# Where a 128x1024 scan stands in VectorE's order of the attention stage

## What is computed

```
x = x + mamba(layernorm(x))
x = x + moe(layernorm(x))
x = x + attention(layernorm(x))
x = x + moe(layernorm(x))
```

```
phi_q = elu(q) + 1 ; phi_k = elu(k) + 1          # q, k, v = x @ Wq.T, x @ Wk.T, x @ Wv.T
A   = tril(phi_q @ phi_k.T)                      # inside a chunk
num = A @ v + phi_q @ S_prev                     # S_prev: sum of phi_k.T @ v over earlier chunks
den = A.sum(-1) + phi_q . Z_prev + 1e-6          # Z_prev: sum of phi_k over earlier chunks
y   = (num / den) @ Wp.T + bp
```

## Time and profile before

| | |
|---|---|
| time, median of 3 runs | 3362.16 us (3361.99 to 3362.63) |
| profiled execution, own time | 3362.63 us |
| its span | 3360.8 us |
| PE busy | 2712.3 us (81%) |
| DVE busy | 2302.4 us (69%) |
| ACT busy | 1717.8 us (51%) |
| POOL busy | 2124.2 us (63%) |
| chain that ended last | PE 40%, POOL 24%, DVE 23%, issue 8%, ACT 3% |
| turns 1 to 14 of attention | 2363 to 2857 us of the span |

### The profile page before, as it was taken

One profiled execution on the slowest core, in us unless ns is written; L12 is line 12 of the kernel. 1 busy time (PEld: TensorE's weight loads), 2 busy tenths in 40 slices (PEclk: granted clock), 3 DMA queues, 4 the chain that ended last, 5 costly groups with the idle time before them and its releaser, 6 DMA issues.

```text
span 3360.8 us, 54089 instructions
## 1 busy us (share of the span) xinstructions
PE 2712.3 (81%) x20202; PEld 1495.0 (44%) x20202; DVE 2302.4 (69%) x2483; ACT 1717.8 (51%) x3115; POOL 2124.2 (63%) x1317
## 2 busy tenths in 40 slices
PE   5787788887888778887754499996999999359998
PEld 2233334333343333343332266554666666235665
DVE  1799999999999999999996522213666666552211
ACT  3677777777777777777751122223444443122221
POOL 1899999999999999999992054433333232124442
PEclk9899999988999889998876699998999999679999
DMA  3456565565566655666542033332111111213442
GB/s 112 103 127 155 137 144 133 140 145 140 140 138 146 146 134 132 144 149 143 133 107 60 13 90 71 83 51 59 46 46 40 52 46 38 67 28 87 89 89 25
DMA packets 227392, 330.01 MB, mean 98 GB/s; under 512 B 40546, under 2 KB 116834, under 8 KB 227011
## 3 DMA queue, kind: packets, MB, share of 16 engines
q1 hardware_dynamic: 202562, 292.49, 35.3%
q0 software_dynamic: 24576, 34.10, 6.0%
HBM read 240.52 MB, written 85.98 MB: 97 GB/s over the span
## 4 chain that ended last, share of the span: by engine, by line
PE 40%; POOL 24%; DVE 23%; issue 8%; ACT 3%; DMA 1%; SPq 0%; DVEq 0%; POOLq 0%; ACTq 0%
POOL m_side L584 14%; DVE m_pair L668 8%; POOL m_hc L593 7%; PE g_h L1341 6%; PE f_h L1341 6%; PE t_wb L2056 6%; DVE m_hc L668 5%; PE f_yp L1355 3%; PE m_wk L771 3%; PE g_yp L1355 3%; DVE m_hc L677 2%; PE t_num L2056 2%; PE m_y L863 2%; PE m_pair L919 2%; DVE t_am L1978 2%
## 5 line engine op out<-in xcount | busy, mean ns | idle before, releaser
L584 POOL TENSOR_TENSOR m_side<-m_du_r,m_bc 128x1024 f32<-128x1024 f32 x416 | 975.0, 2368 | 13.4 <-DMA m_du_r<-ddd 13.1
L351 ACT ACTIVATE m_pair<-m_delta_r,m_a_neg 128x512 f32<-128x512 f32 x832 | 539.7, 681 | 179.0 <-DVE m_hc L677 128.6
L593 POOL TENSOR_TENSOR m_hc<-m_hc,m_bc 128x1024 f32<-128x1024 f32 x208 | 492.2, 2370 | 99.6 <-DVE m_hc L668 97.9
L668 DVE TENSOR_TENSOR_SCAN m_pair<-m_pair,m_side 128x1024 f32<-128x1024 f32 x240 | 547.9, 2283 | 3.4 <-ACT m_pair L351 2.8
L863 PE MATMUL m_y<-m_hc,m_fold 128*32 128x512 f32 x2048 | 321.5, 702 | 229.8 <-DVE m_hc L677 121.2
L668 DVE TENSOR_TENSOR_SCAN m_hc<-m_pair,m_side 128x1024 f32<-128x1024 f32 x176 | 397.7, 2275 | 28.6 <-ACT m_pair L351 28.6
L677 DVE TENSOR_TENSOR m_hc<-m_pair,m_bc 128x1024 f32<-128x1024 f32 x304 | 370.5, 1219 | 7.3
L771 PE MATMUL m_wk<-m_xnT,m_w_in 128*128 128x512 f32 x512 | 276.9, 668 | 10.8 <-DVE m_cw_diag L725 10.0
L771 PE MATMUL m_wk<-m_xs,m_cw_diag 128*128 128x512 f32 x512 | 244.1, 605 | 15.5 <-ACT m_xs L416 15.5
L919 PE MATMUL m_pair<-m_b_diag,m_du_t 128*32 128x128 f32 x6144 | 203.8, 289 | 43.5 <-DVE m_hc L668 24.3
L919 PEld LDWEIGHTS m_pair<-m_b_diag,m_du_t 128*32 128x32 f32 x6144 | 179.0, 117 | 124.7 <-issue 123.4
(11 more groups left out here) (308 smaller groups left out, 4887.4 us busy)
## 6 DMA issues: line engine op xcount, KB each, us to landing
m_delta_r<-ddd SPq DMA_DIRECT2D x256, 256.0 KB, 6.8
m_du_r<-ddd SPq DMA_DIRECT2D x256, 256.0 KB, 7.7
m_bc<-bcd SPq DMA_DIRECT2D x256, 128.0 KB, 2.9
ddd<-m_delta SPq DMA_DIRECT2D x32, 512.0 KB, 3.2
ddd<-m_du SPq DMA_DIRECT2D x32, 512.0 KB, 4.1
f_w<-in_w SPq DMA_DIRECT2D x24, 512.0 KB, 6.1
g_w<-in_w SPq DMA_DIRECT2D x24, 512.0 KB, 6.1
m_xt<-in_x SPq DMA_DIRECT2D x16, 512.0 KB, 10.9
```

What stands on the lines that cost most here:

```text
L351: last = nc.scalar.activation(to, delta_r[:, c % 2, q, :], ACT.Exp, scale=a_neg[:, c * NQ + q, st:st + 1])
L584: nc.gpsimd.tensor_tensor(side[:, un % RING, :, :], du_r[:, c % 2, 2 * h:2 * h + 2, :], bc[:, 0, st:st + 1, :].to_broadcast([P, 2, T]), AL ...
L593: nc.gpsimd.tensor_tensor(hc[:, un % RING, :, :], hc[:, un % RING, :, :], bc[:, 1, st:st + 1, :].to_broadcast([P, 2, T]), ALU.mult).then_i ...
L668: nc.vector.tensor_tensor_scan(to, decay, added, 0.0, ALU.mult, ALU.add).then_inc(S["scan"], 1)
```

## The change

In DVE's body of the attention stage, the call of `sum_keys` for the next batch is moved ahead of the calls of `phi` for m = 2 and 3. Its own waits (for phi of m = 0 and 1 of that batch, and for POOL's product of the batch before) go with it.

```diff
                     out_stats(b - 1, 1 - par)
                 mask(b, 1)
                 if not last:
+                    sum_keys(b + 1, 1 - par)
                     phi(b + 1, 1 - par, 2)
                     phi(b + 1, 1 - par, 3)
-                    sum_keys(b + 1, 1 - par)
                 keep2(b)
                 if ahead(b):
                     in_stats(b + 2, par)
```

## The result

The changed kernel takes 3399.7 us (median of 4 runs, 3393.35 to 3407.66), against 3362.39 for the kernel before beside it (3361.99 to 3366.5): 37.3 us more, a ratio of 1.0113 with a 95% interval of 1.01 to 1.0128. The forecast was 3402, with a range of 3393 to 3416. The four runs of the kernel before lie within 4.5 us and those of the changed one spread over 14. The record has 36 unprofiled executions of the changed kernel in all, from 3393.35 to 3410.71 us with a median of 3401.9; the twelve shortest have a mean granted clock of 0.909 over the whole execution, the twelve longest of 0.904. So the clock seems to have a part in the spread.

The account below looks back on a forecast made before the run. It took DVE's phi of slice 2, which releases PE's value matmuls in each attention turn, as the bound. Delay of 32.0 us (30.7 + 1.3) plus 8 us of clock made 40 us more: 3402 us, range 3393 to 3416.

Parts of the forecast that it names:

- The bound: In every attention turn, the start of phi of slice 2 on DVE sets when PE goes on; turns take 35.28 us.
- The delay: The scan delays phi 2 and PE's values by 2.19 us in turns 1 to 14, 1.28 in turn 0: 32.0 us.
- The second rival: A later wait in the turn partly absorbs the delay; at half the delay 3378 us, chance 0.07.
- Phi 3, the mask of block 2 and z times q at no cost: Behind the moved scan on DVE and POOL: phi 3 covered by 1.2 us, z times q by 4, mask's return worth 0.
- The clock: PE's gap before the values grows to 3.33 us; the clock falls in five turns at 1.64 us each: 8 us.
- the first rival: The delay in attention without any fall of PE's clock: 3394 us, chance 0.17.
- Third rival: PE's clock falls in every one of the 14 turns: 3417 us, or 3440 with low stretches twice as long; chance 0.13.

Follow-up runs that it names:

- e9: Changed kernel with half the scan ahead of phi 2, half behind phi 3, and four unread matmuls before the values in turns 1 to 14: 3376.8 us against 3361.13.
- e10: Against e8, the scan moved behind the mask of the state and the input norm's statistics: 3362.57 us against 3362.85 for the kernel before.
- e12: The order of e10 in turns 1 to 13 only, the kernel before's order in turns 0, 14 and 15: 3365.5 us against 3375.22 for the kernel before.
- e8: Kernel before with the output norm's four statistics instructions in pairs ahead of and behind phi 2, their aggregation ahead of the scan: 3376.23 us, ratio 1.0049.
- e3: Changed kernel with the scan put between phi 2 and phi 3: 3399.32 us, 1.0046 of the kernel before.
- e2: Changed kernel with four unread matmuls on PE ahead of the values in turns 1 to 14: 3415.09 us, 1.0092 of the kernel before.
- e1: The changed kernel again, unaltered, on a chip with long expert stages: 3423.14 us against 3384.12 for the kernel before.
- e4: Changed kernel with the scan cut in two, half ahead of phi 2 and half behind phi 3: 3414.64 us, 1.0092 of the kernel before.
- e11: The changed kernel again, unaltered, on a chip without the long expert stages: 3398.96 us against 3362.85 for the kernel before.
- e6: Kernel before with the output norm's statistics moved behind phi 3, ahead of the scan: 3417.65 us, ratio 1.0171.
- e7: Against the kernel before, scan and output statistics change places: scan ahead of the mask of block 1, statistics behind phi 3: 3385.51 us, ratio 1.0067.

## Why the prediction held, step by step

**The bound: right.** Phi of slice 2 sets when PE goes on. It shows from both sides: what delays phi 2 lengthens each turn by the delay (37.46 in the changed kernel, 36.40 in e9), and what makes it earlier shortens the turn (e10 and e12), as long as the scan doesn't hold POOL (e8). e3 leaves phi 2 alone and keeps the 1.14 us.

**The delay: right to 1 us.** 2.19 us a turn were charged and 2.18 found, turn 0's gap came out at 1.63 us for 1.64, and e2 measured the whole at 31.0 us for 32.0 (32.4 in its profiled attention stage). The second rival (partly absorbed) is out: PE's later waits of 0.33, 0.28, 0.35 and 0.44 us in turn 7 are the same to 0.01 us in both kernels.

**Phi 3, the mask of block 2 and z times q at no cost: right.** In the changed kernel none of the waits for them grew. That phi 3 had 1.2 us to spare is borne out by e3: there it starts 2.2 us further behind phi 2 than in the changed kernel, and 1.06 us of it reach the turn. The mask of block 2 came 0.2 us sooner relative to the values and not 0.3 to 0.5, for it now waits for PE; its worth of 0 stands.

**The clock: the right mechanism, about the right total, wrong number and price.** The term was five turns x 1.64 = 8 us. The runs show three, three and four turns, at 1.4 to 2.8 us each: 5.7, 5.8 and 7.2 us in the three profiles, 8.0 as e1 less e2. Fewer falls, each dearer, since the low stretch reaches past the values into the next matmuls in some turns; that the two errors cancel in part is luck, and five was a choice between none and 14. The spread of the times fits this term: the fastest of the four runs, 3393.35, is 31.0 us over the kernel before, which is the delay without a fall (the first rival's 3394), and the slowest 45.3. But these runs have no profile, so it is argued and not shown. Third rival: the clock did not fall in every turn. By the rule of the Trainium skill (TensorE: Matmul & The Clock Gate, Why this matters for your kernels) it should have; the trace disagrees, with a full clock after 11 of 14 gaps of 3.3 us. Where the step was weak is in its reason, that a gap "just below the one that fell" makes a fall a matter of length. The rows it compared don't carry that. Windows of the kernel before, over the first stage's gap of 3.38 us itself and over a longer stretch behind the gap of 4.08 us:

```profile
176.40:179.70 3.30, 0.00 (x0) 0.02 (x1) 3.27 (x3) 1.20 (x3) 3.30 (x2) 0.61 1.05 199
...
193.50:197.50 4.00, 3.62 (x28) 2.22 (x32) 3.97 (x3) 4.00 (x10) 4.00 (x2) 0.59 0.44 131
```

The clock behind the 3.38 us had already fallen early in the gap (0.61 on average over it). Behind the 4.08 us it fell as well, after the 0.7 us that the prediction looked at: 1.00 there, 0.59 over 4 us. And e4's gaps of 2.26 us fell in 8 of 14 turns, and equal gaps in one kernel did both. What else decides, these runs leave open. The profiles show 0 of 14 at 0.36, 0.53, 1.14, 1.6 (with fill) and 1.75 us, 8 of 14 at 2.26, 3 or 4 at 3.32, 14 of 14 at 5.5. I expected a rise with length and there is none between the middle ones. The turns aren't independent draws either: the falls come in two turns running (all eight of e4; 11 and 12, 8 and 9, 1 and 2, 11 and 12 in the changed kernel), but for turn 1 in two of its profiles.

**POOL: a term left out, without effect on the sum.** The prediction said that no POOL instruction moves by itself and counted for POOL only z times q. Its z times q was right (it starts 0.6 us behind the values, 0.8 predicted). But in the changed kernel POOL's 128x4 product on line 1713 falls beside the scan. The line as a group, in the kernel before:

```profile
L1713 POOL TENSOR_TENSOR t_nm<-t_nm,t_rstd x32: 200/200/209, 2288.9 to 2878.6; 128x4 f32<-128x4 f32 x32
```

and in the changed one (shortest, median and longest, in ns):

```profile
L1713 POOL TENSOR_TENSOR t_nm<-t_nm,t_rstd x32: 200/202/2277, 2298.9 to 2926.7; 128x4 f32<-128x4 f32 x32
```

In turn 2 it starts and ends with the scan (2420.52 to 2422.79). Timeline of POOL there, and of ACT, which takes the result:

```profile
2419.30 1.04 POOL L1711 TENSOR_TENSOR t_rstd<-t_ve,t_nhalf 128x4 f32<-128x4 f32 x1 [0.18 <-POOL t_nm L1709]
2420.52 2.27 POOL L1713 TENSOR_TENSOR t_nm<-t_nm,t_rstd 128x4 f32<-128x4 f32 x1 [0.18 <-POOL t_rstd L1711]
...
2425.95 2.08 ACT L1806 ACTIVATE t_xn1t<-t_xb,t_nm,t_rstd 128x256 f32<-128x256 f32 x4
```

Thirteen of its 32 executions, one in each of turns 2 to 14, take 1.98 to 2.28 us, 26.7 us more together, which is nearly all of the 27.3 us that POOL is busier in attention. (I had expected it in every turn in e11; its profile shows the same thirteen.) With half of the scan in the same place (e4) it takes just over half as long:

```profile
L1713 POOL TENSOR_TENSOR t_nm<-t_nm,t_rstd x32: 198/202/1214, 2300.7 to 2920.5; 128x4 f32<-128x4 f32 x32
```

It costs nothing in the changed kernel, because ACT takes the factors only at 2425.95, 3.2 us after they are ready. In e8 the same thing decided the result, and in e6, against e7 with its statistics as late, it has a large part in it.

## What to carry to other kernels

Before moving a long instruction in an engine's order, find which instruction of that engine another one waits for without slack: here 2.19 us ahead of phi 2 cost 31 us, 2.2 us ahead of phi 3 cost 15, and behind the statistics the scan cost nothing in turns 1 to 13 but 2.2 us in turn 0. Price a new gap on TensorE as a chance, with a range from none to all turns, and not by a threshold in its length; when you read the clock from a row, look inside the gap and well behind it too. Test it by filling the gap with unread matmuls; that splits delay and clock in one run. Look also at what the moved instruction will run beside, on other engines: a tiny instruction can be held for the whole of a long one.

## What the runs showed of the hardware

A small POOL instruction on SBUF that falls beside DVE's scan ends only with the scan: 2.27 us for 0.20 (line 1713, changed kernel), 1.21 us beside the half scan of 1.21 us (e4), 2.00 and 2.11 us for 0.24 (line 1708, e8 and e6), and 0.24 again in e7 and e10, where the scan stands elsewhere. The Trainium skill (SBUF — State Buffer, SBUF: two separate sides) says that VectorE, with two inputs in SBUF, and GpSimd take one pair of ports in turns, each for a whole instruction. The traces agree; the scan reads two tiles in SBUF, and beside the mask, whose one input lies in PSUM, POOL's line 1711 keeps its 1.04 us.

Gaps of the same length on TensorE, in the same place of a loop of equal turns, were followed by a granted clock of 0.50 in some turns and 1.00 in others. In the profiled executions the gap of 2.26 us (e4) brought a fall in 8 of 14 turns, the gap of 3.32 us (changed kernel) in 3, 3 and 4.

Two chips differ by 11 us (459 against 470) in each expert stage, with the same instructions, busy times within 2% and the same granted clock of 0.89; attention shows no such difference (642.5 against 643.1 us in e1 and e11). The cause is open.
